# Layer norms of a two-layer Mamba kernel: one sequence of eight tiles, the correction two tiles behind the centring

## The chip, the cores and the metric

The kernel runs on one core of a Trainium2 chip. The metric is the device time of one execution in microseconds (us); lower is better. Runs of the same kernel are compared on the same chip, and the profile is one further execution of the same program.

## The reference

The input is `x` of shape (2, 2048, 256): two batches of 2048 tokens with 256 features. Two layers run one after the other, and each begins with a layer norm over the features, without scale or shift. The norms are what the change touches; the mixers (selective scans), the mixture of experts and the feed-forward parts are long but stay as they are.

```python
def _layernorm(x, axis=-1, eps=1e-05):
    m = jnp.mean(x, axis=axis, keepdims=True)
    v = jnp.var(x, axis=axis, keepdims=True)
    return (x - m) / jnp.sqrt(v + eps)
...
x = L0_attn_x
xn = _layernorm(x, axis=-1)
x = x + _L0_attn_ref(xn, ...) + _L0_ffn_ref(xn, ...)
xn = _layernorm(x, axis=-1)
x = x + _L1_attn_ref(xn, ...) + _L1_ffn_ref(xn, ...)
return x
```

## The kernel before, in words

`program` runs its stages one after the other, each a block that all engines enter and leave together: `constants`, `layernorm` (the first norm), `mixer0`, `experts0`, at whose end `layernorm` is called a second time, then `mixer1` and `last`. Everything is float32 with features on the partitions: 256 features are C = 2 groups of 128 partitions, and tokens run along the free axis. `acc` holds x, and `k.xn` holds the normalised tokens with a pad of three at each side of a batch.

`layernorm` works on tiles of TT = 512 tokens, PB = 4 tiles in each of B = 2 batches, so eight tiles, numbered i = 4b + q. One tile goes through six steps, which I give letters for the rest of the text:

- M, TensorE line 184: four matmul records form half of the mean in PSUM (`stat`, two slots).
- C, VectorE line 240, two instructions: `xn` = mean/2 - x/2 (centring).
- S, ScalarE line 210: the square of twice that into `sq` (two slots).
- V, TensorE line 193: four matmul records form the variance (`var`, two slots).
- T, ScalarE lines 217, 219 and 221: logarithm, exponential and square, that is the reciprocal root r0 and r2 = r0 squared.
- R, VectorE lines 250 and 254: a Newton step (`ra`, then `rstd`), which the kernel calls `correct`.
- The multiplication, GpSimd line 162, two instructions: `xn` times `rstd`.

The order on each engine is written out by `staggered`. The first half of tile i is followed by the second half of tile i-1, so TensorE runs M(i) V(i-1), ScalarE S(i) T(i-1), VectorE C(i) R(i-1). This is done anew for each batch: after the fourth tile the second half of that tile is finished before the next batch begins. In the first norm the two batches are a hardware loop (`Fori`), so waits and addresses are formed from a register; in the second norm they are written out.

The first norm loads its tiles from DRAM by SyncE (line 139). The four loads of batch 0 start at once, those of batch 1 each wait until C of the tile with the same place in batch 0 is done, since both batches use the same four semaphores.

The second norm has more to do ahead of each tile (class `Combine`). SyncE loads `zp`, 2 MB for each tile, into two slots (line 1117), and a load waits for the products two tiles before. TensorE's `products` P(i) turns expert outputs back into token order (lines 1133 and 1127), ScalarE's `keep` K(i) copies four pieces from PSUM (line 1144), VectorE's `add` A(i) adds the result to `acc` (line 1149), and GpSimd stores the sum to DRAM (line 157) just before it multiplies that tile. `staggered` gives these one tile ahead: TensorE runs P(i+1) M(i) V(i-1), ScalarE K(i+1) S(i) T(i-1), VectorE A(i+1) C(i) R(i-1), but P, K and A of tile 4 come only after the second half of tile 3.

Waits that matter: V(i) waits for S(i) and for R(i-2) (the slot of `var`), M(i) for C(i-2), T(i) for V(i) and R(i-2), S(i) for C(i) and V(i-2), and the multiplication of a tile for its R.

Of the kernel before, what the change touches and what calls it, by code (L numbers as in the profile page):

```python
# [5 lines left out]
ALU = mybir.AluOpType  # L6
ACT = mybir.ActivationFunctionType
# [4 lines left out]
P = 128  # L12
E = 256
C = E // P
B = 2
L = 2048
T = B * L
TT = 512
# [3 lines left out]
PAD = KC - 1  # L22
# [4 lines left out]
EPS = 1e-5  # L27
ds = bass.ds
# [59 lines left out]
def layernorm(nc, k, src, load=None, save=None, before=None):  # L88
# [6 lines left out]
    with ExitStack() as ctx:  # L95
        m = Mem(nc, ctx, "ln" if load is not None else "ln1")
        stat, var = m.ps("mean", [P, 2, TT]), m.ps("var", [P, 2, TT])
# [8 lines left out]
        loaded = [m.sem(f"loaded{q}") for q in range(PB)] if load is not None else None  # L106
        if before is not None:
            before.place(m)
        block = ctx.enter_context(nc.Block())

        def over_batches(engine, body):

            if before is None:
                with engine.Fori(0, B) as b:
                    body(b)
            else:
                for b in range(B):
                    body(b)

        def staggered(first_half, second_half, ahead=None):  # L120


            if ahead is not None:
                ahead(0)
            for q in range(PB):
                if ahead is not None and q + 1 < PB:
                    ahead(q + 1)
                first_half(q)
                if q:
                    second_half(q - 1)  # L130
            second_half(PB - 1)

        @block.sync
        def _(sp):
            if load is not None:
                def body(b):
                    for q in range(PB):
                        sp.wait_ge(centred, b * (q + 2) + 1)
                        sp.dma_start(src[:, :, ds(b * L + q * TT, TT)],
                                     load.rearrange("(c p) t -> p c t", p=P)[:, :, ds(b * L + q * TT, TT)]  # L140
                                     ).then_inc(loaded[q], 16)
                over_batches(sp, body)
            if before is not None:
                def body(b):
                    for q in range(PB):
                        before.load(sp, b * PB + q, b * (PB // 2) + q // 2, q % 2)
                over_batches(sp, body)

        @block.gpsimd
        def _(pool):  # L150
            pool.sem_inc(normed, 2)
            def body(b):
                for q in range(PB):
                    i = b * PB + q
                    if save is not None:
                        pool.wait_ge(before.added, 2 + (i + 1))
                        pool.dma_start(save.rearrange("(c p) t -> p c t", p=P)[:, :, ds(b * L + q * TT, TT)],
                                       src[:, :, ds(b * L + q * TT, TT)]).then_inc(saved, 16)
                    pool.wait_ge(newton, 4 + 2 * i + 2)
                    for c in range(C):  # L160
                        xs = k.xn[:, c, b, ds(PAD + q * TT, TT)]
                        ins = pool.tensor_tensor(xs, xs, rstd[:, q % 2, :], ALU.mult)
                    ins.then_inc(normed, 1)
            over_batches(pool, body)
            if save is not None:
                pool.wait_ge(saved, 16 * B * PB)

        @block.tensor
        def _(pe):
            if before is not None:  # L170
                pe.sem_inc(before.out_ready, 2)
                pe.sem_inc(before.tok_ready, 8)
            pe.sem_inc(var_ready, 2)
            pe.wait_ge(set_up, 1)
            def body(b):
                def means(q):
                    i = b * PB + q
                    if load is not None:
                        pe.wait_ge(loaded[q], b * 16 + 16)
                    if before is not None:  # L180
                        pe.wait_ge(before.added, 2 + (i + 1))
                    pe.wait_ge(centred, i + 1)
                    for c in range(C):
                        mm = pe.matmul(stat[:, q % 2, :], half_mean[:], src[:, c, ds(b * L + q * TT, TT)],
                                       start=c == 0, stop=c == C - 1)
                    mm.then_inc(mean_ready, 1)

                def variances(q):
                    i = b * PB + q
                    pe.wait_ge(squared, i + 1)  # L190
                    pe.wait_ge(newton, 4 + 2 * i - 2)
                    for c in range(C):
                        mm = pe.matmul(var[:, q % 2, :], k.mean[:], sq[:, q % 2, c, :], start=c == 0, stop=c == C - 1)
                    mm.then_inc(var_ready, 1)

                staggered(means, variances, before and (lambda q: before.products(pe, b * PB + q, b * (PB // 2) + q // 2, q % 2)))
            over_batches(pe, body)

        @block.scalar
        def _(act):  # L200
            act.preload_act_table_set("natural_log_exp_and_others")
            act.wait_ge(set_up, 1)
            if before is not None:
                act.sem_inc(before.tok_kept, 2)
            def body(b):
                def squares(q):
                    i = b * PB + q
                    act.wait_ge(centred, 2 + (i + 1))
                    act.wait_ge(var_ready, 1 + i)
                    act.activation(sq[:, q % 2], k.xn[:, :, b, ds(PAD + q * TT, TT)], ACT.Square,  # L210
                                   scale=2.0).then_inc(squared, 1)

                def roots(q):
                    i = b * PB + q
                    act.wait_ge(var_ready, 2 + (i + 1))
                    act.wait_ge(newton, 4 + 2 * i - 2)
                    act.activation(logv[:, q % 2, :], var[:, q % 2, :], ACT.Ln, bias=epst[:, 0:1]).then_inc(logged, 1)
                    act.wait_ge(logged, i + 1)
                    act.activation(r0[:, q % 2, :], logv[:, q % 2, :], ACT.Exp, scale=-0.5).then_inc(root, 1)
                    act.wait_ge(root, i + 1)  # L220
                    act.activation(r2[:, q % 2, :], r0[:, q % 2, :], ACT.Square).then_inc(root_ready, 1)

                staggered(squares, roots, before and (lambda q: before.keep(act, b * PB + q, q % 2)))
            over_batches(act, body)

        @block.vector
        def _(dve):
            dve.memset(epst[:], EPS)
            dve.memset(half_mean[:], 0.5 / E).then_inc(set_up, 1)
            if before is not None:  # L230
                dve.sem_inc(before.added, 2)
            dve.sem_inc(centred, 2)
            dve.sem_inc(newton, 4)
            def body(b):
                def centre(q):

                    i = b * PB + q
                    dve.wait_ge(mean_ready, i + 1)
                    for c in range(C):
                        ins = dve.scalar_tensor_tensor(  # L240
                            out=k.xn[:, c, b, ds(PAD + q * TT, TT)], in0=src[:, c, ds(b * L + q * TT, TT)], scalar=-0.5,
                            in1=stat[:, q % 2, :], op0=ALU.mult, op1=ALU.add)
                    ins.then_inc(centred, 1)

                def correct(q):

                    i = b * PB + q
                    j = q % 2
                    dve.wait_ge(root_ready, i + 1)
                    dve.scalar_tensor_tensor(out=ra[:, j, :], in0=var[:, j, :], scalar=EPS, in1=r2[:, j, :], op0=ALU.add,  # L250
                                             op1=ALU.mult).then_inc(newton, 1)
                    dve.wait_ge(newton, 4 + 2 * i + 1)
                    dve.wait_ge(normed, 1 + i)
                    dve.scalar_tensor_tensor(out=rstd[:, j, :], in0=ra[:, j, :], scalar=-3.0, in1=r0[:, j, :],
                                             op0=ALU.add, op1=ALU.mult).then_inc(newton, 1)

                staggered(centre, correct, before and (lambda q: before.add(dve, b * PB + q, q % 2)))
            over_batches(dve, body)


def scan_counts(it, g):
# [2175 lines left out]
```

## Time and profile before

| | us |
|---|---|
| median of 3 runs | 3595.62 (3590.44 to 3596.41) |
| the profiled execution | 3593.18 |
| its span in the trace | 3591.4 |
| TensorE matmul busy | 2834.1 (79%) |
| VectorE busy | 2831.2 (79%) |
| GpSimd busy | 2260.6 (63%) |
| ScalarE busy | 1825.2 (51%) |
| first norm, from the first load to the last multiplication | 2.1 to 61.0 |
| second norm, from its first load to the last multiplication | 876.3 to 977.9 |

The shares are averages over stages that have different limits, so the two norms, 4.5% of the span together, have to be read on their own: the waits inside a stretch, and the instructions in order of time. PE in a row is TensorE's matmuls, PEld its weight loads, DVE VectorE, ACT ScalarE, POOL GpSimd, SP SyncE. [...]

### The profile page before, as it was taken

The numbers are of one execution on the slowest core, as the hardware profiler recorded it, in microseconds if no ns is written. First come the engines' busy times: TensorE is split into PE (matmuls) and PEld (weight loads), VectorE is DVE, ScalarE is ACT, GpSimd is POOL, SyncE is SP. The second block draws the span as 40 slices with busy tenths as digits, with TensorE's granted clock in tenths as the row PEclk, the third lists the DMA queues.
The fourth block names the chain that finished last, engine by engine and source line by source line (L and its number), as shares of the span: only waits on it lengthen the run. The fifth ranks groups of instructions, "written<-read, shape, count | busy, mean of one in ns | idle before, by whom it ended". The sixth has DMA issues, their size and how long they took to land. (4 is left out here: it accounts for less than half of the span.)

```text
span 3591.4 us, 25524 instructions
## 1 busy us (share of the span) xinstructions
PE 2834.1 (79%) x7878; PEld 1199.1 (33%) x7878; DVE 2831.2 (79%) x2234; ACT 1825.2 (51%) x2455; POOL 2260.6 (63%) x1086
## 2 busy tenths in 40 slices
PE   5677677675657888888788798797897887689899
PEld 2222222354223333333333233233333333244344
DVE  4899799653359999999999999999999999355300
ACT  4677477332355655555655565655555554233311
POOL 3499199201229889899899899898898888100000
PEclk7799799988879989989999999999999999899899
DMA  1011011156514444545454555545545556301000
GB/s 58 16 52 48 7 47 53 40 188 237 174 64 175 165 169 165 177 164 175 172 182 164 178 176 169 174 160 181 178 169 178 181 171 205 101 24 36 12 18 24
DMA packets 164647, 451.39 MB, mean 126 GB/s; under 512 B 23328, under 2 KB 52192, under 8 KB 164480
## 3 DMA queue, kind: packets, MB, share of 16 engines
q1 hardware_dynamic: 158752, 428.79, 34.9%
q0 software_dynamic: 5760, 20.97, 1.5%
q8 instruction: 63, 1.03, 0.1%
q14 instruction: 72, 0.59, 0.1%
HBM read 414.85 MB, written 34.87 MB: 125 GB/s over the span
## 5 line engine op out<-in xcount | busy, mean ns | idle before, releaser
L1408 POOL TENSOR_TENSOR mix_prod<-mix_spread,mix_h 128x1024 f32<-128x1024 f32 x512 | 1375.4, 2688 | 236.5 <-DVE mix_h L1814 129.9
L1908 PE MATMUL mix_banks<-mix_prod,kept_ident 128*128 128x512 f32 x2048 | 1040.6, 634 | 81.5 <-POOL mix_prod L1408 55.6
L1458 ACT ACTIVATE mix_side_in<-mix_dt,mix_neg_a 128x1024 f32<-128x1024 f32 x384 | 437.6, 1141 | 317.6 <-DVE mix_h L1814 314.2
L1908 PEld LDWEIGHTS mix_banks<-mix_prod,kept_ident 128*128 128x128 f32 x2048 | 402.3, 201 | 513.5 <-issue 298.2
L1800 DVE TENSOR_TENSOR mix_banks<-mix_banks,mix_dtu 128x1024 f32<-128x1024 f32 x384 | 467.1, 1216 | 7.6 <-POOL mix_dtu L1398 3.9
L1814 DVE TENSOR_TENSOR_SCAN mix_h<-mix_side_in,mix_state,mix_banks 128x1024 f32<-128x1024 f32 x192 | 450.6, 2347 | 18.5 <-ACT mix_side_in L1458 0.9
L1898 PE MATMUL mix_banks<-mix_parts,kept_sel 96*128 96x512 bf16 x768 | 246.2, 404 | 264.1 <-DVE mix_h L1814 256.1
L1814 DVE TENSOR_TENSOR_SCAN mix_h<-mix_side_in,mix_banks 128x1024 f32<-128x1024 f32 x192 | 438.9, 2286 | 18.8 <-ACT mix_side_in L1458 1.3
L436 POOL TENSOR_TENSOR mix_drive<-mix_drive,mix_du 128x1024 f32<-128x1024 f32 x128 | 306.9, 2414 | 90.8 <-ACT mix_drive L503 90.1
L1418 POOL TENSOR_TENSOR mix_side_in<-mix_spread,mix_dtu 128x512 f32<-128x512 f32 x256 | 339.1, 1325 | 0.1
L655 DVE TENSOR_TENSOR_SCAN mix_h<-mix_banks,mix_state,mix_drive 128x1024 f32<-128x1024 f32 x128 | 296.3, 2340 | 32.4 <-ACT mix_banks L509 27.6
L1450 ACT ACTIVATE mix_state<-mix_h 128x1 f32<-128x1 f32 x256 | 51.7, 202 | 410.0 <-DVE mix_h L1814 409.2
L1898 PEld LDWEIGHTS mix_banks<-mix_parts,kept_sel 96*128 96x128 bf16 x768 | 59.2, 101 | 558.3 <-DVE mix_h L1814 452.7
L1458 ACT ACTIVATE mix_banks<-mix_dt,mix_neg_a 128x1024 f32<-128x1024 f32 x128 | 142.0, 1109 | 124.4 <-DVE mix_h L1814 123.9
L769 PE MATMUL mix_banks<-mix_prod,kept_ident 128*128 128x512 f32 x352 | 178.6, 632 | 10.7 <-DVE mix_turn L673 10.7
L509 ACT ACTIVATE mix_banks<-mix_turn,mix_neg_a 128x1024 f32<-128x1024 f32 x128 | 141.6, 1106 | 60.9 <-DVE mix_h L655 44.7
L2228 DVE TENSOR_TENSOR fin_base<-fin_banks,fin_base 128x512 f32<-128x512 f32 x16 | 10.3, 685 | 205.0 <-PE fin_banks L2300 205.0
L503 ACT ACTIVATE mix_drive<-mix_dd,mix_mask 128x1024 f32<-128x1024 f32 x128 | 145.0, 1133 | 15.2 <-DVE mix_turn L614 15.2
L1814 DVE TENSOR_TENSOR_SCAN mix_h<-mix_banks,mix_state,mix_side_in 128x1024 f32<-128x1024 f32 x64 | 149.3, 2333 | 0.0
L1814 DVE TENSOR_TENSOR_SCAN mix_h<-mix_banks,mix_side_in 128x1024 f32<-128x1024 f32 x64 | 145.4, 2272 | 0.0
L867 POOL DMA_DIRECT2D slot_outputs<-exa_inter x32 | 17.3, 539 | 203.1 <-DVE exa_inter L981 198.4
L1670 DVE SCALAR_TENSOR_TENSOR mix_u<-mix_x,mix_taps,mix_u 128x1024 f32<-128x1024 f32 x96 | 122.8, 1281 | 14.3 <-ACT mix_u L1487 14.0
(258 smaller groups left out, 4381.1 us busy)
## 6 DMA issues: line engine op xcount, KB each, us to landing
mix_spread<-c_rows SPq DMA_DIRECT2D x640, 512.0 KB, 3.8
mix_c_row<-c_rows SPq DMA_DIRECT2D x40, 512.0 KB, 3.6
exa_f<-f SPq DMA_DIRECT2D x32, 512.0 KB, 7.0
slot_outputs<-exa_inter POOLq DMA_DIRECT2D x32, 512.0 KB, 7.1
ln_zp<-slot_outputs SPq DMA_DIRECT2D x8, 2048.0 KB, 9.9
first_acc<-xT SPq DMA_DIRECT2D x8, 512.0 KB, 3.5
x_scratch<-first_acc POOLq DMA_DIRECT2D x8, 512.0 KB, 3.7
fw_scratch<-mix_res SPq DMA_DIRECT2D x8, 512.0 KB, 6.3
```

The lines of the kernel that those rows point to most:

```text
L436: pool.tensor_tensor(r.drive[:, i % 3, :], r.drive[:, i % 3, :], part(du, i // NS), ALU.add).then_inc(r.drive_ready, 1)
L503: act.activation(r.drive[:, i % 3, :], part(dd, i // NS), ACT.Copy, scale=mask[:, at:at + 1]).then_inc(mask_ready, 1)
L509: act.activation(decay[i % 2], part(dt, i // NS), ACT.Exp, scale=neg_a[:, at:at + 1]).then_inc(r.decay_ready, 1)
L655: dve.tensor_tensor_scan(r.h[:, i % 3, :], decay[i % 2], r.drive[:, i % 3, :], state[:, at:at + 1], ALU.mult, ALU.add).then_inc(r.scan_don ...
L769: mm = pe.matmul(y_bank[:, q, :], which, r.prod[:, i % 2, q * TT:(q + 1) * TT], start=i % NS == 0, stop=True, skip_group_check=True)
L1408: pool.tensor_tensor(prod[:, un % 2, :], spread[:, i % SLOTS, :], h[:, un % HR, :], ALU.mult).then_inc(prod_ready, 1)
L1418: ins = pool.tensor_tensor(half(side_in[:, 2, :], hf), half(spread[:, i % SLOTS, :], hf), half(dtu[:, g % MB, :], hf), ALU.mult)
L1458: act.activation(drive[un % 2] if pooled(un) else side_in[:, un % 2, :], dt[:, at // NS, :], ACT.Exp, scale=neg_a[:, way(p), at:at + 1]).t ...
L1800: dve.tensor_tensor(drive[un % 2], drive[un % 2], dtu[:, at // NS, :], ALU.mult).then_inc(drive_ready, 1)
L1814: dve.tensor_tensor_scan(h[:, un % HR, step], a_in[:, step], b_in[:, step], state[:, at:at + 1] if p % NC else 0.0, ALU.mult, ALU.add).the ...
L1898: mm = pe.matmul(half(drive[un % 2], hf), k.sel[:, at % NS, :], half(parts[:, p % 2, :], hf), start=True, stop=True)
L1908: mm = pe.matmul(y_bank[:, hf, :], k.ident[:], half(prod[:, un % 2, :], hf), start=False, stop=True, skip_group_check=True)
```

## The change

- `staggered` runs over the eight tiles of both batches as one sequence, in both norms. On no engine is there a place any more where the fourth tile is finished before the fifth begins.
- `staggered` takes a `lag`. VectorE uses 2 and so runs C(i) R(i-2); TensorE and ScalarE stay at 1.
- In the second norm P, K and A of tile 4 now come ahead of the first half of tile 3, as for every other tile.
- The hardware loop of the first norm is gone; its instructions are written out for both batches.
- The first norm has eight load semaphores in place of four, and the wait ahead of each load is gone, so all eight loads are issued one after the other at the start.

```diff
-        def staggered(first_half, second_half, ahead=None):
+        tiles = [(b, q) for b in range(B) for q in range(PB)]
+
+        def staggered(first_half, second_half, ahead=None, lag=1):
             if ahead is not None:
-                ahead(0)
-            for q in range(PB):
-                if ahead is not None and q + 1 < PB:
-                    ahead(q + 1)
-                first_half(q)
-                if q:
-                    second_half(q - 1)
-            second_half(PB - 1)
+                ahead(*tiles[0])
+            for i in range(len(tiles) + lag):
+                if ahead is not None and i + 1 < len(tiles):
+                    ahead(*tiles[i + 1])
+                if i < len(tiles):
+                    first_half(*tiles[i])
+                if i >= lag:
+                    second_half(*tiles[i - lag])
...
-                def body(b):
-                    for q in range(PB):
-                        sp.wait_ge(centred, b * (q + 2) + 1)
-                        sp.dma_start(src[:, :, ds(b * L + q * TT, TT)],
-                                     load.rearrange("(c p) t -> p c t", p=P)[:, :, ds(b * L + q * TT, TT)]
-                                     ).then_inc(loaded[q], 16)
-                over_batches(sp, body)
+                for b, q in tiles:
+                    sp.dma_start(src[:, :, b * L + q * TT:b * L + (q + 1) * TT],
+                                 load.rearrange("(c p) t -> p c t", p=P)[:, :, b * L + q * TT:b * L + (q + 1) * TT]
+                                 ).then_inc(loaded[b * PB + q], 16)
...
-                staggered(centre, correct, before and (lambda q: before.add(dve, b * PB + q, q % 2)))
-            over_batches(dve, body)
+            staggered(centre, correct, before and (lambda b, q: before.add(dve, b * PB + q, q % 2)), lag=2)
```

## Rows read from the trace of the kernel before

**Rows 1.** Waits by engine and line, 0 to 62 us: us in total, times, longest.

```profile
DVE ln_ra L250 <- ACT ln_r L221: 25.5, 8, 4.4
```

**Rows 2.** Timeline, first norm, one tile's round: start, duration, then the idle before.

```profile
20.23 1.06 ACT L210 ACTIVATE ln_sq<-kept_xn 128x1024 f32 x1 [2.77 <-DVE kept_xn L240]
21.20 0.67 ACT L217 ACTIVATE ln_logv<-ln_var,ln_eps 128x512 f32<-128x512 f32 x1
...
23.22 0.69 DVE L250 SCALAR_TENSOR_TENSOR ln_ra<-ln_var,ln_r 128x512 f32<-128x512 f32 x1 [3.11 <-ACT ln_r L221]
...
24.56 1.27 DVE L240 SCALAR_TENSOR_TENSOR kept_xn<-first_acc,ln_mean 128x512 f32 x2
...
25.96 1.06 ACT L210 ACTIVATE ln_sq<-kept_xn 128x1024 f32 x1 [2.77 <-DVE kept_xn L240]
```

**Rows 3.** Timeline, first norm, where the first batch ends and the second begins.

```profile
27.15 3.77 PE L193 MATMUL ln_var<-ln_sq,kept_mean 128*128 128x512 f32 x4 [3.75 <-ACT ln_sq L210]
...
30.72 4.62 PE L184 MATMUL ln_mean<-first_acc,ln_half_mean 128*128 x8
...
34.46 2.48 DVE L240 SCALAR_TENSOR_TENSOR kept_xn<-first_acc,ln_mean 128x512 f32 x4
```

**Rows 4.** Timeline, TensorE in the first norm, two steps back to back.

```profile
14.66 1.88 PE L184 MATMUL ln_mean<-first_acc,ln_half_mean 128*128 x4
...
16.37 1.88 PE L193 MATMUL ln_var<-ln_sq,kept_mean 128*128 128x512 f32 x4
```

**Rows 5.** Timeline, GpSimd at the end of the first norm.

```profile
58.50 2.48 POOL L162 TENSOR_TENSOR kept_xn<-kept_xn,ln_rstd 128x512 f32 x2 [1.67 <-DVE ln_rstd L254]
```

**Rows 6.** DMA issues of the page: count, KB each, median us to landing.

```profile
first_acc<-xT SPq DMA_DIRECT2D x8, 512.0 KB, 3.5
```

**Rows 7.** Busy us by stretch: PE, PEld, DVE, ACT, POOL, clock, DMA share, GB/s.

```profile
25.00:30.00 5.00, 2.85 (x4) 1.31 (x5) 1.85 (x4) 2.89 (x4) 1.96 (x2) 0.59 0.29 105
```

**Rows 8.** Timeline, TensorE in the last stage, 32 matmuls without a pause.

```profile
3545.54 13.89 PE L2300 MATMUL fin_banks<-fin_g,fin_down 128*128 128x512 f32 x32
```

**Rows 9.** Timeline, second norm, one tile's round, each engine's rows in its answer.

```profile
904.54 1.88 PE L184 MATMUL ln_mean<-first_acc,ln_half_mean 128*128 128x512 f32 x4
...
913.78 1.88 PE L184 MATMUL ln_mean<-first_acc,ln_half_mean 128*128 128x512 f32 x4
...
906.46 1.29 DVE L240 SCALAR_TENSOR_TENSOR kept_xn<-first_acc,ln_mean 128x512 f32<-128x512 f32 x2 [0.49 <-PE ln_mean L184]
...
908.74 0.67 ACT L217 ACTIVATE ln_logv<-ln_var,ln_eps 128x512 f32<-128x512 f32 x1
...
910.64 0.64 ACT L1144 ACTIVATE ln_tok<-ln_by_token 128x256 f32<-128x256 f32 x2
```

**Rows 10.** Timeline, TensorE in the second norm, between the two batches.

```profile
923.76 3.60 PE L193 MATMUL ln_var<-ln_sq,kept_mean 128*128 128x512 f32 x4 [2.95 <-ACT ln_sq L210]
927.29 1.07 PE L1133 MATMUL ln_by_token<-ln_zp,exp_perm_t 128*32 128x256 f32 x16
```

**Rows 11.** Timeline, second norm, TensorE of the sixth tile and later.

```profile
947.76 1.88 PE L184 MATMUL ln_mean<-first_acc,ln_half_mean 128*128 128x512 f32 x4
...
958.35 1.88 PE L184 MATMUL ln_mean<-first_acc,ln_half_mean 128*128 128x512 f32 x4
...
968.34 3.50 PE L193 MATMUL ln_var<-ln_sq,kept_mean 128*128 128x512 f32 x4 [2.96 <-ACT ln_sq L210]
```

**Rows 12.** Timeline, GpSimd at the end of the second norm.

```profile
975.43 2.46 POOL L162 TENSOR_TENSOR kept_xn<-kept_xn,ln_rstd 128x512 f32<-128x512 f32 x2 [0.54 <-DVE ln_rstd L254]
```

**Rows 13.** Loads of the second norm: one issue of SyncE's timeline, and landing times.

```profile
913.06 0.36 SPq L1117 DMA_DIRECT2D ln_zp<-slot_outputs  x1
...
DMA to landing us min/median/max: 7.8/9.9/12.8
```

**Rows 14.** One line's instructions (ns minimum, median, maximum), and a group of the page.

```profile
L254 DVE SCALAR_TENSOR_TENSOR ln_rstd<-ln_ra,ln_r x16: 691/692/693, 18.2 to 974.6; 128x512 f32<-128x512 f32 x16
...
L1408 POOL TENSOR_TENSOR mix_prod<-mix_spread,mix_h 128x1024 f32<-128x1024 f32 x512 | 1375.4, 2688 | 236.5 <-DVE mix_h L1814 129.9
```

More of the change, by code:

```diff
@@ L105, in layernorm @@
         logged, newton, normed, saved = m.sem("logged"), m.sem("newton"), m.sem("normed"), m.sem("saved")
-        loaded = [m.sem(f"loaded{q}") for q in range(PB)] if load is not None else None
+        loaded = [m.sem(f"loaded{i}") for i in range(B * PB)] if load is not None else None
         if before is not None:
@@ L109, in layernorm @@
         block = ctx.enter_context(nc.Block())
[L111 to L118, printed above, removed]
-        def staggered(first_half, second_half, ahead=None):
-            if ahead is not None:
-                ahead(0)
-            for q in range(PB):
-                if ahead is not None and q + 1 < PB:
-                    ahead(q + 1)
-                first_half(q)
-                if q:
-                    second_half(q - 1)
-            second_half(PB - 1)
+        tiles = [(b, q) for b in range(B) for q in range(PB)]
+        def staggered(first_half, second_half, ahead=None, lag=1):
+            if ahead is not None:
+                ahead(*tiles[0])
[6 more added lines that the diff above has]
+                    second_half(*tiles[i - lag])
         @block.sync
@@ L135, in _ @@
             if load is not None:
-                def body(b):
-                    for q in range(PB):
-                        sp.wait_ge(centred, b * (q + 2) + 1)
-                        sp.dma_start(src[:, :, ds(b * L + q * TT, TT)],
-                                     load.rearrange("(c p) t -> p c t", p=P)[:, :, ds(b * L + q * TT, TT)]
-                                     ).then_inc(loaded[q], 16)
-                over_batches(sp, body)
+                for b, q in tiles:
+                    sp.dma_start(src[:, :, b * L + q * TT:b * L + (q + 1) * TT],
+                                 load.rearrange("(c p) t -> p c t", p=P)[:, :, b * L + q * TT:b * L + (q + 1) * TT]
+                                 ).then_inc(loaded[b * PB + q], 16)
             if before is not None:
[L144 to L147, printed above, removed]
+                for b, q in tiles:
+                    before.load(sp, b * PB + q, b * (PB // 2) + q // 2, q % 2)
         @block.gpsimd
@@ L151, in _ @@
             pool.sem_inc(normed, 2)
[L152 to L164, printed above, removed]
+            for b, q in tiles:
+                i = b * PB + q
+                if save is not None:
+                    pool.wait_ge(before.added, 2 + (i + 1))
+                    pool.dma_start(save.rearrange("(c p) t -> p c t", p=P)[:, :, ds(b * L + q * TT, TT)],
+                                   src[:, :, ds(b * L + q * TT, TT)]).then_inc(saved, 16)
+                pool.wait_ge(newton, 4 + 2 * i + 2)
+                for c in range(C):
+                    xs = k.xn[:, c, b, ds(PAD + q * TT, TT)]
+                    ins = pool.tensor_tensor(xs, xs, rstd[:, q % 2, :], ALU.mult)
+                ins.then_inc(normed, 1)
             if save is not None:
@@ L174, in _, with means, variances @@
             pe.wait_ge(set_up, 1)
[L175 to L197, printed above, removed]
+            def means(b, q):
+                i = b * PB + q
+                if load is not None:
+                    pe.wait_ge(loaded[i], 16)
+                if before is not None:
+                    pe.wait_ge(before.added, 2 + (i + 1))
+                pe.wait_ge(centred, i + 1)
+                for c in range(C):
+                    mm = pe.matmul(stat[:, q % 2, :], half_mean[:], src[:, c, ds(b * L + q * TT, TT)],
+                                   start=c == 0, stop=c == C - 1)
+                mm.then_inc(mean_ready, 1)
+            def variances(b, q):
+                i = b * PB + q
+                pe.wait_ge(squared, i + 1)
+                pe.wait_ge(newton, 4 + 2 * i - 2)
+                for c in range(C):
+                    mm = pe.matmul(var[:, q % 2, :], k.mean[:], sq[:, q % 2, c, :], start=c == 0, stop=c == C - 1)
+                mm.then_inc(var_ready, 1)
+            staggered(means, variances, before and (lambda b, q: before.products(pe, b * PB + q, b * (PB // 2) + q // 2, q % 2)))
         @block.scalar
@@ L204, in _, with squares, roots @@
                 act.sem_inc(before.tok_kept, 2)
[L205 to L224, printed above, removed]
+            def squares(b, q):
+                i = b * PB + q
+                act.wait_ge(centred, 2 + (i + 1))
+                act.wait_ge(var_ready, 1 + i)
+                act.activation(sq[:, q % 2], k.xn[:, :, b, ds(PAD + q * TT, TT)], ACT.Square,
+                               scale=2.0).then_inc(squared, 1)
+            def roots(b, q):
+                i = b * PB + q
+                act.wait_ge(var_ready, 2 + (i + 1))
+                act.wait_ge(newton, 4 + 2 * i - 2)
+                act.activation(logv[:, q % 2, :], var[:, q % 2, :], ACT.Ln, bias=epst[:, 0:1]).then_inc(logged, 1)
+                act.wait_ge(logged, i + 1)
+                act.activation(r0[:, q % 2, :], logv[:, q % 2, :], ACT.Exp, scale=-0.5).then_inc(root, 1)
+                act.wait_ge(root, i + 1)
+                act.activation(r2[:, q % 2, :], r0[:, q % 2, :], ACT.Square).then_inc(root_ready, 1)
+            staggered(squares, roots, before and (lambda b, q: before.keep(act, b * PB + q, q % 2)))
         @block.vector
@@ L233, in _ @@
             dve.sem_inc(newton, 4)
[L234 to L255, printed above, removed]
-                staggered(centre, correct, before and (lambda q: before.add(dve, b * PB + q, q % 2)))
@@ L258, in _, with centre, correct @@
-            over_batches(dve, body)
+            def centre(b, q):
+                i = b * PB + q
+                dve.wait_ge(mean_ready, i + 1)
+                for c in range(C):
+                    ins = dve.scalar_tensor_tensor(
+                        out=k.xn[:, c, b, ds(PAD + q * TT, TT)], in0=src[:, c, ds(b * L + q * TT, TT)], scalar=-0.5,
+                        in1=stat[:, q % 2, :], op0=ALU.mult, op1=ALU.add)
+                ins.then_inc(centred, 1)
+            def correct(b, q):
+                i = b * PB + q
+                j = q % 2
+                dve.wait_ge(root_ready, i + 1)
+                dve.scalar_tensor_tensor(out=ra[:, j, :], in0=var[:, j, :], scalar=EPS, in1=r2[:, j, :], op0=ALU.add,
+                                         op1=ALU.mult).then_inc(newton, 1)
+                dve.wait_ge(newton, 4 + 2 * i + 1)
+                dve.wait_ge(normed, 1 + i)
+                dve.scalar_tensor_tensor(out=rstd[:, j, :], in0=ra[:, j, :], scalar=-3.0, in1=r0[:, j, :],
+                                         op0=ALU.add, op1=ALU.mult).then_inc(newton, 1)
```

## The prediction

> **What bounds the kernel now.** The page's busy shares come first and say little here: the two norms are 4.5% of the span. All stages follow one another through barriers, so time saved inside a norm comes off the whole, unless it only turns into another wait inside that norm. So I read the two norms alone: first the waits by engine, then the instructions in order of time, to find which loop sets the distance between tiles.
>
> In the first norm the largest wait of an engine that others depend on is VectorE before R, for ScalarE: 25.5 us in eight times [rows 1]. The timeline shows the loop. S starts at 20.23, T at 21.20, R at 23.22, the next C only at 24.56, behind R on VectorE, and the next S at 25.96 [rows 2]. So the round is C, S, T of the tile before, R of the tile before, and again C: 25.96 - 20.23 = 5.73 us a tile. TensorE isn't in it: M takes 16.37 - 14.66 = 1.71 us from start to start and V the same, 3.43 us a tile [rows 4], and it waits 3.75 us before a V [rows 3]. [...]
>
> Between the batches there is a seam. V(3) starts at 27.15, M(4) only behind it at 30.72, and C(4) at 34.46, against 24.56 for C(3) [rows 2, 3]: 9.90 us instead of 5.73.
>
> The second norm has another round, since P and K run ahead. M(1) starts at 904.54, C(1) at 906.46, T(0) at 908.74, K(3) at 910.64, and M(2) at 913.78 once K has fed the rest of P [rows 9]: 9.24 us. R isn't in it; it sits in VectorE's idle time before the next A. The seam is there too: V(3) at 923.76 after 2.95 us of waiting, P(4) only behind it at 927.29 [rows 10].
>
> **First norm, part by part.** C(i) no longer stands behind R(i-1). What is late next is TensorE. Measured from M(i)'s start, C(i) starts 1.92 later (906.46 - 904.54, [rows 9]), ends 1.28 after that, S ends about 1.1 later, at 4.3. V(i) stands on TensorE behind M(i), V(i-1) and M(i+1), so at 3 x 1.71 = 5.15. S is in time. R(i-2), now behind C(i), ends at 1.92 + 1.28 + 1.4 = 4.6, with a handoff 4.8: this is the new wait of V(i), and it has 0.3 us to spare. ScalarE's S and T need 3.0 us a tile (20.23 to 23.22, [rows 2]), VectorE's C and R 2.7, GpSimd's multiplication 2.5 [rows 5]. [...]
>
> The start stays as it is up to M(2) at 14.66 [rows 4]. Then come V(1) at 16.37, M(3) 18.09 and so on, to M(7) at 14.66 + 10 x 1.715 = 31.8 and V(6) at 33.5. C(7) is at 31.8 + 1.92 = 33.7 to 35.0, R(5) ends at 36.4, V(7) runs from 36.5 to 38.4. T(7) then takes 2.0 (to 40.5), R(7) 1.4 (to 41.9), and the multiplication runs from 42.2 to 44.7. Before, it ended at 58.50 + 2.48 = 61.0 [rows 5]. The sum is **-16.3 us**. Bounds: V(7) waits about a microsecond and may fall to the low clock, and one round may miss its 0.3 us in every tile, together +3.3, so -13; the other way, no register work for waits gives at most 0.3, so -16.6.
>
> The loads: eight of 512 KB, median 3.5 us to landing [rows 6]. Even one after another at that price the last lands at 2 + 8 x 3.5 = 30 us, before M(7) at 31.8. I put them at nothing; TensorE's rounds are their cover, and without it M would wait for each. SyncE has nothing else queued. The written-out loop costs nothing I can find, as the second norm is written out already.
>
> **Second norm, part by part.** The round stays C, S, T, K, P, M. What goes is the seam: P(4) follows V(1) at 917.3 instead of 927.29. From M(2) at 913.78 to M(6) there are four rounds. The shortest is 9.24 [rows 9]; the one before M(6), 958.35 - 947.76 = 10.59 [rows 11], has part of its work at the low clock. I take two of each, which puts M(6) at 953.4 instead of 958.35: -4.9. Loads allow it: load 5 was issued at 913.06, landing takes 7.8 to 12.8 [rows 13], and P(5) would start at 926.5.
>
> The tail from M(6) on: C(7) doesn't stand behind R(5), so S(7) comes at +6.7, R(5) ends at +8.1, V(7) starts at +8.3 where it now starts at 968.34 - 958.35 = +10.0 [rows 11]. T(7), R(7) follow as before. The store of tile 7 stands on GpSimd behind the multiplication of tile 6, which waits for R(6), now one C later; I put the end of the last multiplication at +17.8, against 975.43 + 2.46 - 958.35 = +19.5 [rows 11, 12]. That is -1.7. Sum **-6.6 us**. Bounds: four rounds of 10.59 and -1.4 give -3.7; four of 9.24 and -2.0 give -9.7.
>
> Together -22.9 us. The profiled execution of 3593.18 (span 3591.4) would become 3570.3 (3568.5). The median of the runs stands 2.4 above that execution, so **3572.7 us**. The bounds are -16.7 and -26.3; with 3 us for the spread of the runs, 3566 to 3582.
>
> **The rivals.**
>
> 1. The second norm gives nothing: each round meets the low clock (4 x 10.59 makes M(6) 956.1), and a load or a store takes the rest, since the loads no longer have the seam to catch up in and the stores move closer together. For it: landings of up to 12.8 us [rows 13] and a round of 10.59 exist. Against: the 9.24 was measured with loads in flight, and P(6), at about 935.7, stands 13 us behind the issue of its load at the end of P(4). 3595.6 - 16.3 = 3579.3.
>
> 2. R's second instruction and the multiplication get in each other's way. It reads `ra` and `r0`, both in SBUF, and all 16 take 691 to 693 ns [rows 14], but none of them meets a multiplication in time in the kernel before; after the change they are close: 0.69 + 0.2 + 2.5 = 3.4 us of 3.43. For it: GpSimd's 128x1024 product takes 2688 ns beside a busy VectorE [rows 14], where two of 128x512 take 2.48 us [rows 5]. At the two tails R(7) would wait about 0.8 us for the end of the multiplication of tile 6, and six rounds could lose 0.3 each: 1.6 to 3.4 us, so about 3575.5. [...]
>
> 3. The lag does little, and only the seams go. If something I don't see keeps 5.73 a tile, the first norm gives 9.90 - 5.73 = 4.2 and the second about 5: 3586.5. Against: the gap before R is in every round, and C has no other reason to be late.
>
> [...]
>
> **How the numbers follow.** Chances: forecast 0.56, rival 1 0.16, rival 2 0.16, rival 3 0.08, rival 4 0.04. The predicted time is the forecast's. The range 3565 to 3583 takes in the forecast with its bounds and rivals 1 and 2 and leaves out 3 and 4. A measurement of this kernel can tell about 0.2%, 7.2 us, from no change: rival 3 lies near that line, so half of it and a little of rival 1 counts as the same. Faster 0.91, same 0.06, slower 0.03.
>
> **What the profile after would show.** Right: in the first norm C(i) some 3.4 us apart from tile 2 on, TensorE without idle time from 12.8 to 35 at clock 1.00, R(i-2) directly behind C(i), the last multiplication ending near 44.7 instead of 61.0 us. In the second norm P(4) directly behind V(1), near 917, and the stage about 6 to 7 us shorter. Wrong: VectorE again waiting for ScalarE before each R, V waiting for R, M for a load, 3.77 us steps in the middle, or R's second instruction longer than 0.7 us beside a multiplication. Any change of length in the stages behind the norms would be outside this sum.

## The result

| | before | after |
|---|---|---|
| median of 8 runs, same chip, us | 3590.84 (3584.95 to 3596.41) | 3571.78 (3563.68 to 3578.46) |
| ratio | | 0.9942, 95% interval 0.9927 to 0.9958 |
| span of the profiled execution, us | 3591.4 | 3570.2 |

By the ratio the change saves 20.8 us (15 to 26); the two medians differ by 19.1. The forecast was 22.9 us less and 3572.7 us. Each experiment below was run beside the kernel before on the same chip, and its ratio is to that; the experiments and the repeated profiles come from three chips. Two single executions, of 14721 us (the kernel before, beside experiments 1 to 3) and of 7155 us (experiment 8), stand far outside all others and are in no ratio. To see where the time went I cut each span at the starts of ScalarE's table loads, which open the blocks, and at the first load of the experts' stage. After the change, for one, these rows of ScalarE and their like stand at 1.79, 44.27, 865.85 and 964.49 us:

```profile
44.27 1.28 ACT L433 ACT_TABLE_LOAD   x1 [4.94 <-PEq L95]
```

Two profiles of each kernel, and a third of before (experiment 7), each a single execution:

| us | first norm | mixer 0 | experts | second norm | the rest |
|---|---|---|---|---|---|
| before | 59.5 | 607.7 | 207.0 | 104.0 | 2611.4 |
| before, repeated | 59.5 | 607.6 | 210.0 | 107.9 | 2614.8 |
| before, once more | 59.7 | 610.3 | 213.2 | 101.6 | 2597.2 |
| after | 42.5 | 610.5 | 211.1 | 98.6 | 2605.7 |
| after, repeated | 42.4 | 607.5 | 218.5 | 99.9 | 2605.5 |

The first norm is 17.0 to 17.3 us shorter, and repeats within 0.2 us. The second is on average 104.5 before and 99.3 after, 5.2 us less. Experiments 3 to 6 add one execution each. Taken together, the four with the old order in the second norm take 101.6 to 107.9 us there (mean 103.9), the five with the new one 97.8 to 100.9 (mean 99.2). The stages that were not touched move by more than that from one execution to the next (experts 207 to 218, the rest 2597 to 2615), which is why the total has an interval of 11 us and the reading has to go by stage.

### The profile page after: what moved, and what is told of

Its sections match the earlier page's. It is cut to its first block and busy times, and to the rows that moved or that the text cites. A ratio compares the mean times of both kernels' runs of the same rounds, so it can differ in the third digit from the quotient of the medians.

```text
span 3570.2 us, 25379 instructions
## 1 busy us (share of the span) xinstructions
PE 2829.8 (79%) x7878; PEld 1199.4 (34%) x7878; DVE 2828.6 (79%) x2234; ACT 1824.7 (51%) x2455; POOL 2258.0 (63%) x1086
## 5 line engine op out<-in xcount | busy, mean ns | idle before, releaser
L846 POOL DMA_DIRECT2D slot_outputs<-exa_inter x32 | 17.3, 539 | 207.3 <-DVE exa_inter L960 202.2
```

## The profile after

The first norm's timeline: three tiles' M and V on TensorE, and what VectorE and GpSimd do in the last of them (start, duration, and in brackets the idle time before and its releaser). It answers to [rows 2] and [rows 4].

```profile
23.78 1.88 PE L168 MATMUL ln_mean<-first_acc,ln_half_mean 128*128 128x512 f32 x4
...
25.49 1.88 PE L177 MATMUL ln_var<-ln_sq,kept_mean 128*128 128x512 f32 x4
...
27.21 1.88 PE L168 MATMUL ln_mean<-first_acc,ln_half_mean 128*128 128x512 f32 x4
...
28.93 1.88 PE L177 MATMUL ln_var<-ln_sq,kept_mean 128*128 128x512 f32 x4
29.13 1.28 DVE L220 SCALAR_TENSOR_TENSOR kept_xn<-first_acc,ln_mean 128x512 f32<-128x512 f32 x2 [0.82 <-PE ln_mean L168]
...
30.33 0.68 DVE L230 SCALAR_TENSOR_TENSOR ln_ra<-ln_var,ln_r 128x512 f32<-128x512 f32 x1
```

M follows M after 3.43 us, V lies between, and no bracket stands behind a TensorE row: TensorE sets the distance. C starts 1.92 after its M, and R directly behind C, with no wait for ScalarE.

The waits of the first norm, 0 to 46 us (us in total, times, longest), against [rows 1] and [rows 3]:

```profile
DVE kept_xn L220 <- PE ln_mean L168: 14.8, 8, 7.1
...
DVE ln_ra L230 <- ACT ln_r L203: 2.8, 2, 1.7
...
PE ln_var L177 <- DVE ln_rstd L234: 1.1, 1, 1.1
```

VectorE's 25.5 us of waiting for ScalarE before R are 2.8, both at the end, after the last C. The new wait, V for R, is there once, at V(7). TensorE's granted clock (a share of full speed), 0.59 at 25 to 30 us in [rows 7], is 1.00:

```profile
25.00:30.00 5.00, 5.00 (x13) 2.28 (x12) 3.45 (x6) 4.37 (x7) 3.71 (x4) 1.00 0.00 0
```

The end of the first norm (GpSimd's row 41.48 answers to [rows 5]):

```profile
38.37 2.48 POOL L148 TENSOR_TENSOR kept_xn<-kept_xn,ln_rstd 128x512 f32<-128x512 f32 x2 [0.63 <-DVE ln_rstd L234]
...
40.08 1.32 DVE L234 SCALAR_TENSOR_TENSOR ln_rstd<-ln_ra,ln_r 128x512 f32<-128x512 f32 x1
41.48 2.47 POOL L148 TENSOR_TENSOR kept_xn<-kept_xn,ln_rstd 128x512 f32<-128x512 f32 x2 [0.63 <-DVE ln_rstd L234]
```

R's second instruction takes 1.32 us where all 16 took 0.69 before [rows 14]: it meets a running multiplication (38.37 to 40.85).

The second norm, M(2), M(6) and V(7), TensorE's timeline, against [rows 9] and [rows 11]:

```profile
904.48 1.88 PE L168 MATMUL ln_mean<-first_acc,ln_half_mean 128*128 128x512 f32 x4
...
945.23 1.96 PE L168 MATMUL ln_mean<-first_acc,ln_half_mean 128*128 128x512 f32 x4
...
953.41 1.96 PE L177 MATMUL ln_var<-ln_sq,kept_mean 128*128 128x512 f32 x4 [1.08 <-DVE ln_rstd L234]
```

Four rounds take 40.75 us (44.57 before). From M(1) on, the five rounds are 9.24, 10.46, 10.64, 9.24 and 10.41. Busy time by round (PE, PEld, DVE, ACT, POOL, granted clock, DMA share, GB/s) shows why they differ:

```profile
895.00:904.50 9.50, 7.45 (x51) 3.21 (x52) 2.51 (x3) 4.21 (x8) 0.00 (x0) 1.00 0.65 221
904.50:915.00 10.50, 8.58 (x51) 3.26 (x50) 3.80 (x5) 4.21 (x8) 2.86 (x3) 0.84 0.72 252
915.00:925.60 10.60, 8.60 (x50) 3.23 (x50) 3.80 (x5) 4.21 (x8) 2.83 (x3) 0.84 0.71 247
925.60:934.80 9.20, 7.14 (x50) 2.90 (x49) 3.80 (x5) 4.21 (x8) 2.83 (x3) 1.00 0.80 281
934.80:945.20 10.40, 8.48 (x50) 3.37 (x49) 3.80 (x5) 4.20 (x8) 2.83 (x3) 0.84 0.15 55
```

The long rounds are those at clock 0.84, with TensorE's same work taking 1.1 to 1.5 us more. In every round TensorE stands idle once, for K:

```profile
PE ln_out L1106 <- ACT ln_tok L1123: 9.6, 5, 1.9
```

One wait of the kernel before is gone, which the prediction did not see. There P(4) and P(5) ran back to back at the seam, and P(6) then stood waiting for its 2 MB load:

```profile
941.77 1.94 PE L1133 MATMUL ln_by_token<-ln_zp,exp_perm_t 128*32 128x256 f32 x16 [3.16 <-DMA ln_zp<-slot_outputs]
```

All five executions with a seam in the second norm have this wait, 3.0 to 3.6 us (before three times, experiments 2 and 3). Without the seam no P waits for a load after P(2).

## The experiments

**1. VectorE's lag back to 1, all else as after.**

```diff
-            staggered(centre, correct, before and (lambda b, q: before.add(dve, b * PB + q, q % 2)), lag=2)
+            staggered(centre, correct, before and (lambda b, q: before.add(dve, b * PB + q, q % 2)), lag=1)
```

> One sequence of eight tiles and eight free loads stay, but VectorE's correction is again one tile behind (lag 1 in both norms). Theory (the order C before R takes R out of the first norm's round, the seam is a separate, smaller gain): the first norm's tiles are again about 5.7 us apart, its last multiplication ends near 56 us (61.0 before, 44.0 after the change), the second norm keeps its gain but for about 1.5 us at its end, and the whole is about 10 us below the kernel before, ratio 0.997. Rival (only the seams and the early loads matter, the lag nothing): the first norm ends near 44 us and the ratio is 0.994 as with the change.

Measured: ratio 0.9988 (0.9971 to 1.0005). First norm 56.0 us, second 101.3. Three of GpSimd's multiplications in the first norm:

```profile
17.20 2.14 POOL L148 TENSOR_TENSOR kept_xn<-kept_xn,ln_rstd 128x512 f32<-128x512 f32 x2 [15.72 <-DVE ln_rstd L234]
22.84 2.14 POOL L148 TENSOR_TENSOR kept_xn<-kept_xn,ln_rstd 128x512 f32<-128x512 f32 x2 [3.49 <-DVE ln_rstd L234]
...
55.00 2.47 POOL L148 TENSOR_TENSOR kept_xn<-kept_xn,ln_rstd 128x512 f32<-128x512 f32 x2 [1.50 <-DVE ln_rstd L234]
```

They are 5.64 us apart and the last ends at 57.5. So with one sequence in place the lag carries 13.5 us of the first norm's 17, and one sequence with early loads and no hardware loop only 3.5. The split depends on the order of the steps: with the seam left in, the lag is worth 8.4 (56.6 in experiment 4 against 48.2 in experiment 2). Rival 3, which left the lag nothing, falls. In the second norm the stretch from M(6) to the next table load is 21.8 us here and 19.3 with lag 2 (19.2 to 19.5 in six executions with it): 2.5 us, more than the 1.5 expected. The first norm is 3.5 us shorter than in the kernel before and not the 5 expected, and the expected ratio, 0.997, lies just outside the interval.

**2. Lag 2, but each batch finished before the next.**

```diff
-            for i in range(len(tiles) + lag):
...
+            parts = [tiles[:PB], tiles[PB:]]
+            for part in parts:
+                if ahead is not None:
+                    ahead(*part[0])
+                for i in range(len(part) + lag):
...
```

> Lag 2 and the eight free loads stay, but each engine again finishes the fourth tile of a batch before the fifth begins, in both norms. Theory: tiles 3.43 us apart inside a batch; the seam costs 3 us in the first norm (M(4) behind V(3), which waits for S(3) and R(1)), so its last multiplication ends near 47 us; the second norm has its old length of 104 us from table load to table load less at most 2, since R was never in its round. The whole 15 to 16 us below before, ratio 0.9955. Rival (the seams are the main gain): first norm above 52 us, ratio 0.998.

Measured: ratio 0.9975 (0.9958 to 0.9992); first norm 48.2 us, second 98.2. Rounds inside a batch are 3.43. The seam costs 5.7 us, not 3, and the timeline shows what I left out, VectorE's queue:

```profile
23.36 3.60 PE L170 MATMUL ln_mean<-first_acc,ln_half_mean 128*128 128x512 f32 x8
...
26.32 0.97 DVE L236 SCALAR_TENSOR_TENSOR ln_rstd<-ln_ra,ln_r 128x512 f32<-128x512 f32 x1
27.22 2.47 DVE L222 SCALAR_TENSOR_TENSOR kept_xn<-first_acc,ln_mean 128x512 f32<-128x512 f32 x4
...
29.64 3.44 PE L179 MATMUL ln_var<-ln_sq,kept_mean 128*128 128x512 f32 x4 [2.68 <-ACT ln_sq L194]
```

M(4) and M(5) are done, but C(4) stands behind R(2) and R(3) until 27.22 (22.26 after the change), TensorE waits 2.68, and V(4) then takes 3.44, at a mean granted clock of 0.57 from 29.6 to 33.1 us, where the V of a round takes 1.88 at 1.00. The second norm is a surprise the other way: 98.2 us with the seam, no longer than after the change. From M(1) to M(6) it takes 50.1 us with the seam and lag 2, against 49.6 to 51.3 in six executions without a seam. Its seam still has P(6)'s wait for a load, 3.63 us, but with lag 2 V(3) no longer waits 2.95 us for S(3) at the seam [rows 10], but 1.08 for R(1), and it takes 1.95 us where it took 3.60 (at a clock of 0.53 from 923.7 to 927.3 us). The measured total, 9 us (3 to 15), is less than these two stages say (11.3 and about 6); the untouched stages move by more than that, and which one took it stays open.

**3. The first norm as after, the second as before.**

```diff
-            for i in range(len(tiles) + lag):
...
+            parts = [tiles] if before is None else [tiles[:PB], tiles[PB:]]
+            lag = lag if before is None else 1
+            for part in parts:
...
```

> The first norm as after the change, the second norm in the order of the kernel before (lag 1, finished after each batch). Theory: the first norm ends at 44 us, the second takes 104 us from table load to table load against 98.6 with the change; 17 us below before, ratio 0.9953. Rival (the second norm brings nothing that lasts): its stage also takes 99 us.

Measured: ratio 0.9957 (0.9941 to 0.9974), 15.4 us. First norm 42.7 us, second 101.9. The first norm is as forecast. The second norm's 101.9 lies between theory (104) and rival (99). The kernel before itself takes 101.6 to 107.9 there, so one profile was too few to expect 104 from, and 101.9 is still above all five executions with the new order.

**4. The second norm as after, the first in its old order, but written out and with free loads.** The edit is that of experiment 3 with the two cases exchanged.

> The second norm as after the change; the first norm in the order of the kernel before (finished after each batch, lag 1 on VectorE), but written out and with eight free loads. Theory (written-out loops and early loads bring little, the order brings the rest): the first norm takes 58 to 59.5 us from table load to table load, the second 97.8 to 100.9 as with the change; 4 to 6 us below before, ratio 0.9985. Rival (the loop's removal is a large part of the first norm's gain): the first norm below 55 us.

Measured: ratio 0.9972 (0.9949 to 0.9996). First norm 56.6 us, second 98.6. Written-out code and early loads are worth 2.9 us in the first norm; the prediction had put this at 0.3 at most, and the theory here at 1.5. The start shows a third of it:

```profile
5.62 6.17 PE L171 MATMUL ln_mean<-first_acc,ln_half_mean 128*128 128x512 f32 x8 [5.62 <-DMA first_acc<-xT]
...
11.89 1.98 PE L180 MATMUL ln_var<-ln_sq,kept_mean 128*128 128x512 f32 x4
```

M(0) starts at 5.62 instead of 6.07 and V(0) at 11.89 instead of 12.84. C(3) is then 1.45 us ahead of the kernel before (23.11 against 24.56, [rows 2]), C(4) 1.7 (32.73 against 34.46, [rows 3]), C(7) 2.2 and the next block 2.9: the rounds take 5.64 instead of 5.73, the seam and the second batch give 0.7 and the end another 0.7. Beside experiment 1 this also prices the seam of the first norm at lag 1: 56.6 - 56.0 = 0.6 us, against 5.7 at lag 2 (experiment 2).

**5. The loads of the second batch held back as before.**

```diff
+                    if b:
+                        sp.wait_ge(centred, q + 3)
                     sp.dma_start(src[:, :, b * L + q * TT:b * L + (q + 1) * TT],
```

> After the change, but each load of the second batch again waits until C of the tile in the same place of the first batch is done. Theory (the early loads hide nothing that was exposed): M(0) starts at 5.4 us, no M waits for a load, the first norm ends at 44.0 to 44.3 us as with the change. Rival (eight loads at once are part of the gain): TensorE waits before M(4) or later, and the first norm ends 1 us or more later.

Measured, in one execution: first norm 42.6 us, M(0) at 5.47. No M but the first waits for a load:

```profile
PE ln_mean L170 <- DMA first_acc<-xT: 5.5, 1, 5.5
```

The early loads hide nothing that was exposed. They even took 8.7 us in the median to land (3.5 before, [rows 6]; 3.7 here), which nobody waits for. So what experiment 4 showed comes from writing out the loop, not from the free loads: the first load is issued at 1.80 us in both experiments and at 2.13 in the kernel before. That it is the register work which costs the rest is argued by elimination; no run takes it apart.

**6. The reciprocal root of the first norm in PSUM.** R's second instruction has then one operand in SBUF instead of two; nothing else changes.

```diff
-        logv, r0, r2, ra, rstd = (m.sb(n, [P, 2, TT]) for n in ("logv", "r0", "r2", "ra", "rstd"))
+        logv, r2, ra, rstd = (m.sb(n, [P, 2, TT]) for n in ("logv", "r2", "ra", "rstd"))
+        r0 = (m.ps if before is None else m.sb)("r0", [P, 2, TT])
```

> After the change, but in the first norm the reciprocal root r0 lies in PSUM instead of SBUF, so R's second instruction has one SBUF operand in place of two. Theory (two SBUF operands make it wait for a GpSimd multiplication that is running): the last R's second instruction takes about 0.69 us instead of 1.32 us and the first norm ends 0.6 us earlier, near 43.3 us; in the second norm, left as it was, it still takes about 1.4 us. Rival (it is long for another reason, such as a slot that is not free or the read of the variance): still 1.3 us in both norms.

The last R of the first norm, and of the second norm, which was left alone:

```profile
38.57 4.96 POOL L149 TENSOR_TENSOR kept_xn<-kept_xn,ln_rstd 128x512 f32<-128x512 f32 x4 [0.55 <-DVE ln_rstd L235]
...
40.28 0.69 DVE L235 SCALAR_TENSOR_TENSOR ln_rstd<-ln_ra,ln_r 128x512 f32<-128x512 f32 x1
...
961.46 1.45 DVE L235 SCALAR_TENSOR_TENSOR ln_rstd<-ln_ra,ln_r 128x512 f32<-128x512 f32 x1
```

Both R's second instructions start while GpSimd multiplies. In the first norm it now takes 0.69 us instead of 1.32, and in the second, where both operands stay in SBUF, 1.45. From the start of that instruction to the next block's table load it is 3.6 us instead of 4.2. This is one execution, and experiment 9 repeats it (0.69 us and a first norm of 41.9). It shows rival 2's meeting and its price, 0.6 to 0.8 us at each norm's end, and that R's second instruction pays it with both operands in SBUF (1.32 and 1.45 us) and not with one (0.69).

**7. Both kernels a second time, and before a third.** No edit.

> The changed kernel a second time, for how far the stages move from one execution to the next. Theory (the first norm is deterministic, the stages with large transfers are not): first norm 42.5 us from table load to table load within 0.3, second norm 98.6 within 2, the stretch between the norms 821.5 within 6, the rest 2605.7 within 6. Rival (the stages repeat and the differences between kernels are effects of the change): all within 1 us.

> The kernel before, a second time, to see how far its stages move. Theory (the experts' stage and the long scans behind the second norm vary from one execution to the next, whatever the norms do): first norm 59.5 us from table load to table load within 0.5, the experts' stage anywhere from 207 to 218 us. Rival (the shorter first norm gives something back in the experts' stage, which took 207.0 us in the one profile of before and 209 to 218.5 us in eight others): 207 us within 1.5 again.

> The kernel before, a third time, for the same question. Theory: the experts' stage between 207 and 218 us, and in at least one of the two repeats above 210. Rival: 207 us within 1.5 in both. The second norm 104 us in its one profile: theory says 101 to 105 again.

Measured: the table above. The first norm repeats. The second norm, expected at 101 to 105 us, takes 101.6 in one repeat and 107.9, outside, in the other. The experts' stage takes 207.0, 210.0 and 213.2 us with the kernel before. The suspicion that a shorter first norm gives something back there falls, on few profiles: after the change it is 211.1 and 218.5, in the other kernels with the short first norm 207.6 to 217.6. Mixer 0 has two lengths, 607.3 to 607.9 and 610.2 to 610.6, in both kernels.

**8. ScalarE further behind in the second norm: K(i+1), S(i-1), T(i-2).**

```diff
-            staggered(squares, roots, before and (lambda b, q: before.keep(act, b * PB + q, q % 2)))
+            if before is None:
+                staggered(squares, roots)
+                return
+            before.keep(act, 0, 0)
+            for i in range(len(tiles) + 2):
+                if i + 1 < len(tiles):
+                    before.keep(act, i + 1, (i + 1) % 2)
+                if 1 <= i <= len(tiles):
+                    squares(*tiles[i - 1])
+                if i >= 2:
+                    roots(*tiles[i - 2])
```

> After the change, and in the second norm ScalarE too runs further behind: K(i+1), then S(i-1), then T(i-2), in place of K(i+1) S(i) T(i-1). Theory (the second norm's round is C, S, T, K, the rest of P, M, because K stands behind S and T on ScalarE, and R isn't in it): K no longer waits for C, the rounds fall from 9.24 to 10.6 us to about 7.7 to 8.5, where TensorE's own work or the 2 MB loads decide, the second norm takes about 92 us from table load to table load instead of 98.6, and the whole is about 6 us faster than the change, ratio 0.9925 to the kernel before. Rival (the 2 MB loads set the distance in the second norm): rounds stay above 9 us with TensorE waiting for the load, ratio 0.994.

Measured: ratio to before 0.9927 (0.9905 to 0.9949). Second norm 85.4 us instead of 98.6, every round 7.40 us:

```profile
899.34 1.88 PE L168 MATMUL ln_mean<-first_acc,ln_half_mean 128*128 128x512 f32 x4
...
906.74 1.88 PE L168 MATMUL ln_mean<-first_acc,ln_half_mean 128*128 128x512 f32 x4
...
936.32 1.88 PE L168 MATMUL ln_mean<-first_acc,ln_half_mean 128*128 128x512 f32 x4
```

```profile
907.00:914.00 7.00, 6.80 (x47) 2.62 (x46) 3.74 (x5) 3.93 (x9) 2.65 (x3) 1.00 0.87 301
914.00:922.00 8.00, 7.80 (x52) 3.31 (x52) 4.08 (x6) 4.92 (x9) 3.04 (x4) 1.00 0.91 294
922.00:929.00 7.00, 6.79 (x49) 2.79 (x48) 3.53 (x5) 3.93 (x9) 2.83 (x3) 1.00 1.04 347
```

TensorE is busy for 97% or more of each stretch, no P waits for K or, after P(2), for a load, and the clock stays at 1.00. The round I read before the change, C, S, T, K, P, M, was the right one. Taking K out from behind S and T takes 13 us off this stage, more than twice what the change got there, 9.2 of it by the shorter chain (9.24 to 7.40, five times) and the rest because no round falls below 1.00 (three of the change's five were at 0.84). The expectation had 92 us. It had the ratio almost exactly, 0.9925, but that is no confirmation: with 13 us off the stage instead of 6 the ratio should have been near 0.9905, which is the edge of the measured interval. By the whole time of this version alone a gain over the change isn't shown, as the two intervals overlap; the stage shows it, here and in experiment 9.

**9. Experiments 6 and 8 together.**

> ScalarE one tile further behind in the second norm, and the reciprocal root of the first norm in PSUM, together. Theory: the first norm 0.6 us shorter than with ScalarE's edit alone (42.2 us from table load to table load), the second 85.4 us with rounds of 7.40 us; ratio to before 0.9905 to 0.993, about 14 us faster than the change. Rival (the second norm's 85.4 us were a lucky execution with fast loads): it takes above 92 us here and the ratio is above 0.994.

Measured: ratio to before 0.9902 (0.9885 to 0.9920), median 3560.49; first norm 41.9 us, second 85.2. The theory holds for the second norm and the whole; the first norm is 0.9 us shorter than in experiment 8, 0.6 expected. This version is faster than both kernels: its interval lies below that of the change (0.9927 to 0.9958), each ratio being to the kernel before on its own chip.

## Why the prediction was right

**The whole.** The stages give 17.0 + 5.2 = 22.2 us, close to the 22.9 forecast; the runs say 20.8. That 3572.7 was met within 1 us is partly luck: the three runs it started from had a median of 3595.62, the eight of the result 3590.84, and this error of 4.8 us and the saving put 2 to 4 us too high nearly cancel.

**The bound of the first norm: right.** R was in the round, and TensorE took over at 3.43 us, at clock 1.00 from 12 us on. From M(2) to M(7) the trace after has 17.16 us (30.64 - 13.48), the prediction 17.15. V(7) waits for R(5) and starts 4.7 us after M(7), as worked out. Experiment 1 shows that the lag is what does it.

**Its ends: two terms mis-sized, in opposite directions.** The start up to M(2) I took over unchanged at 14.66; it is 13.48. Experiment 4 finds that in the written-out code (M(2) at 13.71); "no register work gives at most 0.3" was wrong, since experiment 4 has 2.9 us in the whole stage with its old order. From M(2) to the end of the last multiplication I had 30.0 and it took 30.5: the prediction set rival 2's wait at 0.8 and outside the forecast, and it is there with 0.6. So 1.2 us came out better and 0.4 worse. Sum: -17.0 against -16.3.

**The second norm: right in kind, 5.2 against 6.6, and its two terms mis-sized.** For the seam I had 4.9 us. From M(1) to M(6) the four executions with a seam and lag 1 (before three times, and experiment 3) take 51.0 to 55.1, on average 53.0, and the six without a seam, their ScalarE as in the change, 49.6 to 51.3, on average 50.3: 2.7 us. The step that failed is how the seam was read, as one long distance with ordinary rounds around it. At the seam M(3) follows M(2) at once, since no P stands between, and catches up part of what P(4) loses. TensorE's idle time for K is also shorter there, 0.5 to 1.4 us at P(4) and none at P(5), against 1.9 in every round. Against that stands P(6)'s wait of 3.2 us for its load, a part of the seam's cost that the prediction left out. The same holds in the first norm: C(4) is 9.90 us behind C(3), but C(5) follows it at once, as the row at 34.46 with its four instructions in 2.48 us shows [rows 3]; the 4.2 us that rival 3 gave this seam were 0.6. And I took two of four rounds at 9.24 and two at 10.59, a round that ran at a mean clock of 0.84 in the kernel before (947.7 to 958.3 us); after the change, three of five ran at 0.84. And one sequence isn't needed for this gain: with the seam and lag 2 the stretch takes 50.1 (experiment 2), without the seam and at lag 1 49.8 (experiment 1), so either half of the change brings it, and only the seam together with lag 1 is slow. For the tail I had 1.7 and it is 2.4. V(7) takes 1.96 us, at clock 1.00 behind 1.08 us of idle time, where it took 3.50 [rows 11], at 0.57 behind 2.96, 1.5 us that I did not count, and rival 2's wait takes 0.8 of them back (1.45 against 0.69). The first norm's rows have such a V already: 3.77 us, at a clock of 0.50 from 27.1 to 31.0 us, behind 3.75 us of idle time [rows 3]. I did not carry that reading to the last V of the second norm.

**The rivals.** Rival 2 happened in both tails and in no steady round; the steady rounds fit, as 0.69 + 0.2 + 2.5 against 3.43 said they just would. No row of the kernel before has such a meeting; experiment 6 shows that it costs R's second instruction 0.6 to 0.8 us with two operands in SBUF and nothing with one. Rival 3 is refuted by experiment 1. Rival 1 (nothing from the second norm) is refuted by its stage, 97.8 to 100.9 us in five executions against 101.6 to 107.9 in four, though the two ranges come within 1 us of each other. Its premise was the wrong way round as well: the loads had not used the seam to catch up, the seam is where a P waited for one. Rival 4, the slower kernel, did not happen: the clock was 1.00 from 12 us to the end of the first norm's matmuls, and the second norm is shorter. A low clock behind a wait for a transfer stands in the kernel before: behind P(6)'s wait of 3.16 us for a load the granted clock is 0.50 from 941.7 to 946.0 us. The rounds after the change are another case, since TensorE waits in them for ScalarE's K and not for a transfer: with 1.92 us of idle time in each, three of five (four of five in the repeat) ran at about 0.84, and in experiment 8, without that idle time, none did.

**The width.** The range had room for 3 us of spread. The untouched stages spread by 10 and more from one execution to the next; the medians of eight averaged most of that out.

## What to carry to other kernels

In a software pipeline over several engines, write down the round as a closed chain that goes once through each queue; an instruction that merely stands in front of another on its engine is part of it, and moving it one tile back needed no new buffer here, since every tile passed on had two slots already. What it did cost was the meeting of R and the multiplication at the end, 0.6 to 0.8 us. After such a move look at the next queue in the same way: here ScalarE's order was worth more in the second norm than everything the change did there. And price idle time of TensorE twice, once for itself and once for the low clock that can follow it: here a V behind 3.75 us of idle time took 3.77 us, at a clock of 0.50, and one behind 1.08 us took 1.95, at 1.00.

## What the runs showed of the hardware

- R's second instruction on VectorE, with both operands in SBUF, takes 0.69 us alone and 1.32 us (first norm) or 1.45 us (second) beside a running GpSimd multiplication; with one operand in PSUM it stays at 0.69 there (experiments 6 and 9), and C, with one in SBUF, stays at 1.28 to 1.29 for its two beside a multiplication.
- GpSimd's multiplication takes 2.13 to 2.15 us on the tiles of batch 0 and 2.46 to 2.52 us on those of batch 1, in every kernel and in both norms. The instructions differ in nothing but the place of their tile in `xn`; the cause was not tried.
- Eight loads of 512 KB issued together land in 6.7 to 8.7 us in the median (3.5 to 4.3 when spread out), at up to 406 GB/s in one microsecond (11 to 12 us) of the trace after.
- Where TensorE idled 1.92 us in each round, some rounds ran at a mean granted clock of 0.84 and others, alike in their work, at 1.00. Which one falls is not something I could predict from the trace.
- TensorE's work of a round (7.1 to 7.5 us at clock 1.00) takes 8.5 to 8.6 us at a mean clock of 0.84.
